# Patch embedding, attention and a ternary feed-forward layer on one core: the weighted values moved ahead of the column scores in each round

## The chip, the cores and the metric

The kernel runs on one core of one Trainium2 chip. The metric is the device time of one execution in microseconds (us); less is better. Engine names: PE is TensorE (matrix multiply), PEld its weight loads, DVE is VectorE, ACT is ScalarE, POOL is GpSimd, SP is the engine whose queue issues the DMAs.

## The reference

The input is 64 images of 3x224x224 and 64 texts of 32x256. Each image is cut into 196 patches of 16x16x3, each patch is multiplied with a 768x256 matrix, and a bias and a position are added. With the 32 text rows this makes sequences of 228 rows of 256. On them runs one transformer layer, cut here to its core:

```python
h = concatenate([patches(x) @ W_embed + b_embed + pos, txt], axis=1)   # 64 x 228 x 256
n = layernorm(h)
q, k, v = n @ Wq.T, n @ Wk.T, n @ Wv.T                                 # 16 heads of 16
probs = softmax(where(causal, -inf, q @ k.T / sqrt(16)))
h = h + (probs @ v) @ Wo.T + bo
h = h + ternary_linear(gelu(ternary_linear(layernorm(h), w_up)), w_down)   # 256 -> 1024 -> 256
```

A ternary linear layer divides its input by its root mean square and multiplies with the weights' signs, where a weight is over half of the mean absolute weight, and zero elsewhere.

## The kernel before, in words

The 64 images are worked on in 32 pairs. A software pipeline runs over steps t = 0 to 34; in step t pair t is embedded and gets its queries and keys, pair t-1 gets its values and row scores, pair t-2 finishes its attention, and pair t-3 is projected and goes through the feed-forward layer. Steps 3 to 31 have all four stages. A step has eight rounds, k = 0 to 7, and every engine walks through the same rounds with an order written out by hand. There is no planner; only the semaphores tie the engines together.

The attention of a pair is cut into eight groups of four heads. Each group is scored twice:

- **Row scores** (`scores_rows`): queries times keys with the mask added, 16 fp32 matmul instructions on tiles of 32 rows of the array (`score<-km,qm`) and 16 bf16 ones (`score<-cmask,idm`). DVE takes the row maxima from them (`maxima_unit`, L951 and L952).
- **Column scores** (`scores_columns`): the same products transposed, with the maxima folded into the queries, 16 instructions `score<-qm,km`, again on tiles of 32 rows. ACT takes the exponential (`exponential`, L674, tile `pr`), and POOL sets what lies above the diagonal to zero (`causal`, L1155).
- **Weighted values** (`weighted_values`): values times probabilities, 16 instructions `pvps<-pr,vp` with 114 contraction rows and 32 output rows each. Every second round ACT copies the result out (`unscaled`, L741, tile `raw`), DMAs repack it, and DVE divides by the sums (`collect`).

Row and column scores share one PSUM tile, `score`, of four banks. So the column scores of round k wait until DVE has read the row scores of round k, and the row scores of round k+1 wait until the exponential of round k has read the column scores:

```python
eng.wait_ge(*score_emptied(t, k, True))     # columns: v["max"] of this round's rows
eng.wait_ge(*score_emptied(t, k, False))    # rows: a["exp"] of the last columns
```

Everything else that PE does ("dense" work: `pixels`, `embed`, `hidden_rows`, `to_columns`, `queries_keys`, `values`, `projection`, `up`, `down`, `sum_squares`, `maxima_rows`) is laid by hand into the two stretches of a round. The first stretch lies between row scores and column scores, the second between column scores and the next row scores. In steps 3 to 31 they hold:

| round | first stretch | second stretch, behind the weighted values |
|---|---|---|
| 0 | projection | pixels 0 to 2 |
| 1 | values 0, pixels 3 to 5 | embed 0, first half |
| 2 | embed 0, second half, x2t | up 0 to 2 |
| 3 | up 3 to 7 | maxima_rows 0, embed 1 |
| 4 | hidden_rows, values 1 | down, 8 instructions |
| 5 | down, 16 | down, 16 |
| 6 | sum_squares, down, 16 | down, 8, and xt |
| 7 | queries_keys 0 | queries_keys 2 (ahead of the weighted values), maxima_rows 1 |

In round 7 the second half of `queries_keys` (2) needs a PSUM bank that ACT empties (`queries`, L699, tile `qm`). The weighted values of round k belong to the group whose column scores were made in round k-1. They wait for POOL's mask of that group (`p["mask"]`) and, in every second round, for the copy `raw` (`a["raw"]`). The probabilities have two buffers, and the exponential of a group waits for the weighted values of the group two before it. Nearly all matmuls are issued through one helper and appear under its line, L324.

Of the kernel before, what the change touches and what calls it, by code (L numbers as in the profile page):

```python
# [75 lines left out]
def build(nc, x, txt, w_embed, b_embed, pos, wqkvo, bo, w_upT, w_downT, out):  # L76
    with ExitStack() as ctx:
# [116 lines left out]
        def live(pair):  # L194
            return not isinstance(pair, int) or 0 <= pair < NPAIR

        def emptied(pair, name, k):

            m, back = DENSE.index((name, k)) - 3, 0
            while back < 3:  # L200
                if m < 0:
                    m, back = m + NDENSE, back + 1
                other, j = DENSE[m]
                if other != "spare":
                    before = pair + (lag(name, k) - back - lag(other, j))
                    if live(before):
                        if other == "qk":
                            return (a["km"], count(2, before, j // 2 + 1)) if j % 2 else (a["q"], count(4, before, j + 2))
                        return released[other], count(PER[other], before, j + 1)
                m -= 3  # L210
            return a["w"], 1
# [20 lines left out]
        def bank_of(name, k):  # L232
            return dense[:, DENSE.index((name, k)) % 3]
# [88 lines left out]
        def _(eng):  # L322
# [62 lines left out]
            def queries_keys(pair, k):  # L385

                ps = [bank_of("qk", k + j)[:, 0:T2] for j in range(2)]
                w_ = [[[z[:, j, c, (k // 2) * 128:(k // 2) * 128 + 128] for z in wa] for c in range(2)] for j in range(2)]
                if pair == 0 and k == 0:
                    eng.wait_ge(v["wa"], 1)  # L390
                for j in (1, 0):
                    eng.wait_ge(*emptied(pair, "qk", k + j))
                    for c in range(2):
                        if k == 0 and j == 1:
                            eng.wait_ge(a["xt"], count(2, pair, c + 1))
                        mm(ps[j], w_[j][c][0], aT[0][:, c], start=(c == 0), stop=False)
                        mm(ps[j], w_[j][c][1], aT[0][:, c], start=False, stop=False)
                for j in range(2):
                    for c in range(2):
                        if k == 0 and j == 0:  # L400
                            eng.wait_ge(v["xt"], count(2, pair, c + 1))
                        last = mm(ps[j], w_[j][c][0], aT[1][:, c], start=False, stop=(c == 1))
                    last.then_inc(pe["qk"], 1)
# [71 lines left out]
            def scores_columns(t, u, k):  # L475

                pair, q = columns_of(t, k)
                if not live(pair):
                    return
                b, r = divmod(q, 4)  # L480
                m, par = divmod(r, 2)
                buf = u if k < 5 else 1 - u
                if r == 0:
                    eng.wait_ge(v["mq"], count(2, pair, b + 1))

                eng.wait_ge(*score_emptied(t, k, True))
                for kb in range(2):
                    c0 = b * S + kb * R
                    for i in range(4):
                        last = mm(score[0:R, i, kb * S:S + kb * R], km[quad(i), buf, m, par, c0:c0 + R],  # L490
                                  qm[quad(i), par, buf, m, c0:b * S + S], start=True, stop=True,
                                  skip_group_check=True)
                last.then_inc(pe["st"], 1)
# [26 lines left out]
            def weighted_values(pair, par, gi):  # L520

                b, r = divmod(gi, 4)

                eng.wait_ge(p["mask"], count(16, pair, 2 * gi + 2))
                if pair == 0 and gi == 0:
                    eng.wait_ge(v["tbound"], 1)
                if gi == 0:

                    eng.wait_ge(a["v0"], count(2, pair, 2))

                if gi >= 2 and gi % 2 == 0:
                    eng.wait_ge(a["raw"], count(4, pair, gi // 2))
                elif gi == 0 and began(pair - 1):
                    eng.wait_ge(a["raw"], count(4, pair - 1, 4))
                P_ = pr[gi % 2]
                half = r % 2
                for kb in range(2):
                    for i in range(4):
                        last = mm(pvps[quad(i), half * S + kb * R:half * S + S],
                                  vp[:, par + 1 if b else 0, kb, 8 * (r // 2) + 2 * i + half],  # L540
                                  P_[:, i, kb * S:S + kb * R], start=(kb == 0), stop=(kb == 1),
                                  skip_group_check=True)
                last.then_inc(pe["pv"], 1)
# [11 lines left out]
            def step(t, hs):  # L555
                u = hs % 2
                A, Bm, Cc, Dd = live(t), live(t - 1), live(t - 2), live(t - 3)
                for k in range(8):
                    if Bm:
                        scores_rows(t, u, k)  # L560
                    if Dd and k == 0:
                        projection(t - 3)
                    if Bm and k == 1:
                        values(t - 1, 0)
                    if A and k == 1:
                        pixels(t, 3)
                        pixels(t, 4)
                        pixels(t, 5)
                    if A and k == 2:
                        embed(t, 0, 1)  # L570
                    if Dd and k == 2:
                        eng.wait_ge(a["xn2"], count(4, t - 3, 4))
                        to_columns(t - 3, "x2t", 0, xn)
                        to_columns(t - 3, "x2t", 1, xn)
                    if Dd and k == 3:
                        for m in range(3, 8):
                            up(t - 3, m)
                    if A and k == 4:
                        hidden_rows(t, 0)
                        hidden_rows(t, 1)  # L580
                    if Bm and k == 4:
                        values(t - 1, 1)
                    if Dd and k == 5:
                        down(t - 3, 0, 1)
                        down(t - 3, 0, 2)
                    if Dd and k == 6:
                        sum_squares(t - 3)
                        down(t - 3, 1, 1)
                        down(t - 3, 1, 2)
                    if A and k == 7:  # L590
                        queries_keys(t, 0)
                    scores_columns(t, u, k)
                    if A and k == 7:
                        queries_keys(t, 2)
                    pair, gi = (t - 2, k + 2) if k < 6 else (t - 1, k - 6)
                    if live(pair):
                        weighted_values(pair, u if k < 6 else 1 - u, gi)
                    if A and k == 0:
                        pixels(t, 0)
                        pixels(t, 1)  # L600
                        pixels(t, 2)
                    if A and k == 1:
                        embed(t, 0, 0)
                    if Dd and k == 2:
                        up(t - 3, 0)
                        up(t - 3, 1)
                        up(t - 3, 2)
                    if Bm and k in (3, 7):
                        maxima_rows(t - 1, k // 4)
                    if A and k == 3:  # L610
                        embed(t, 1, 0)
                        embed(t, 1, 1)
                    if t == 1 and k == 4:
                        eng.wait_ge(v["tsum"], 3)
                        mm(pvps[:, 0:3], onesf, tern[:, 0:3], start=True, stop=True).then_inc(pe["init"], 1)
                    if Dd and k == 4:
                        down(t - 3, 0, 0)
                    if Dd and k == 5:
                        down(t - 3, 0, 3)
                        down(t - 3, 1, 0)  # L620
                    if Dd and k == 6:
                        down(t - 3, 1, 3)
                    if A and k == 6:
                        eng.wait_ge(a["xn"], count(4, t, 4))
                        to_columns(t, "xt", 0, xn)
                        to_columns(t, "xt", 1, xn)

            steps(step, eng)


# [625 lines left out]
```

## Time and profile before

| | |
|---|---|
| median of 3 runs | 2014.7 us (2012.65 to 2017.67) |
| profiled execution, its own time | 2019.13 us |
| its span, first to last instruction | 2017.4 us |
| mean granted TensorE clock | 0.978 of full speed |
| PE busy | 1927.3 us, 96% of the span |
| PEld busy | 1574.9 us, 78% |
| DVE, ACT, POOL busy | 1465.9, 1312.9, 892.5 us |

All durations come from the profiled execution. A matmul's row in the timeline gives the start of the first instruction of the group, its length to the modelled end of the last, the names out<-in, the count, and, where the engine sat idle before it, how long and what ended the idle time. Modelled ends overlap the next start, so that the time a group takes from PE is read from start to start.

### The profile page before, as it was taken

The numbers are of one execution on the slowest core, as the hardware profiler recorded it, in microseconds if no ns is written. First come the engines' busy times: TensorE is split into PE (matmuls) and PEld (weight loads), VectorE is DVE, ScalarE is ACT, GpSimd is POOL, SyncE is SP. The second block draws the span as 40 slices with busy tenths as digits, with TensorE's granted clock in tenths as the row PEclk, the third lists the DMA queues.
The fourth block names the chain that finished last, engine by engine and source line by source line (L and its number), as shares of the span: only waits on it lengthen the run. The fifth ranks groups of instructions, "written<-read, shape, count | busy, mean of one in ns | idle before, by whom it ended". The sixth has DMA issues, their size and how long they took to land.

```text
span 2017.4 us, 59822 instructions
## 1 busy us (share of the span) xinstructions
PE 1927.3 (96%) x25090; PEld 1574.9 (78%) x25090; DVE 1465.9 (73%) x2717; ACT 1312.9 (65%) x1986; POOL 892.5 (44%) x1067
## 2 busy tenths in 40 slices
PE   4779999999999999999999999999999999999975
PEld 3668888888888888788888888888888888888754
DVE  3667778777777777777777777777777778777753
ACT  3347766666776676767667677666667766667652
POOL 1124444444444544444454444444454445444543
PEclk8789999999999999999999999999999999999987
DMA  5011111111111101111111111111111111010000
GB/s 149 15 46 41 50 55 50 35 45 44 53 50 55 50 27 53 41 55 50 53 47 31 47 49 51 54 50 35 45 45 52 50 55 50 30 51 17 30 29 24
DMA packets 66116, 93.72 MB, mean 46 GB/s; under 512 B 10082, under 2 KB 59718, under 8 KB 65592
## 3 DMA queue, kind: packets, MB, share of 16 engines
q1 hardware_dynamic: 65848, 89.90, 15.6%
q8 instruction: 199, 3.26, 0.7%
q14 instruction: 69, 0.57, 0.1%
HBM read 45.03 MB, written 14.94 MB: 30 GB/s over the span
## 4 chain that ended last, share of the span: by engine, by line
PE 90%; ACT 3%; DVE 3%; issue 2%; POOL 1%; DMA 1%; SPq 0%; DVEq 0%; POOLq 0%; ACTq 0%
PE dense L324 50%; PE score L324 21%; PE pvps L324 9%; PE dense L342 4%; PE dense L381 3%; ACT qm L699 2%; PE dense L552 2%; PE dense L370 1%; POOL acc L1174 1%; DMA borow<-bo 1%; DVE mx L952 1%; ACT pr L674 0%; DVE st L936 0%; DVE mx L951 0%; ACT xn L723 0%
## 5 line engine op out<-in xcount | busy, mean ns | idle before, releaser
L1155 POOL TENSOR_SCALAR_AFFINE_SELECT pr<-pr 114x456 f32<-114x456 f32 x512 | 310.8, 631 | 853.2 <-ACT pr L674 853.2
L674 ACT ACTIVATE pr<-score 114x1368 f32<-114x1368 f32 x256 | 335.6, 1311 | 301.3 <-PE score L324 301.0
L951 DVE TENSOR_REDUCE mx<-score 114x4 f32<-114x456 f32 x256 | 161.1, 629 | 260.3 <-PE score L324 259.7
L952 DVE TENSOR_REDUCE mx<-score 114x4 f32<-114x912 f32 x256 | 281.0, 1098 | 0.0
L324 PE MATMUL dense<-wdn,g 128*114 128x256 bf16 x1024 | 243.4, 283 | 2.0 <-ACT g L683 1.2
L324 PE MATMUL score<-qm,km 32*114 32x228 f32 (+1 forms) x4096 | 221.8, 331 | 18.7 <-DVE mx L952 15.4
L324 PE MATMUL dense<-wdn,gl 128*114 128x256 bf16 x1024 | 236.6, 276 | 0.0
L1174 POOL TENSOR_TENSOR acc<-acc,sq 128x456 f32<-128x456 f32 x192 | 222.4, 1158 | 19.0 <-POOL acc L1174 0.4
L324 PEld LDWEIGHTS score<-qm,km 32*114 32x114 f32 x4096 | 176.0, 175 | 69.4 <-issue 40.5
L324 PE MATMUL score<-km,qm 32*114 32x114 f32 (+1 forms) x4096 | 221.8, 331 | 7.5 <-ACT pr L674 6.7
L324 PE MATMUL pvps<-pr,vp 114*32 114x228 f32 (+1 forms) x4096 | 205.2, 318 | 1.0 <-ACT raw L741 0.6
L908 DVE RECIPROCAL rs<-rs 128x228 f32<-128x228 f32 x128 | 200.5, 1566 | 5.5 <-DMA cx<-raw 5.5
L324 PEld LDWEIGHTS score<-km,qm 32*114 32x114 f32 x4096 | 127.1, 175 | 60.1 <-issue 37.9
L324 PEld LDWEIGHTS pvps<-pr,vp 114*32 114x32 f32 x4096 | 108.5, 110 | 68.9 <-POOL pr L1155 10.9
L683 ACT ACTIVATE g<-dense 128x456 f32<-128x456 f32 x256 | 135.1, 553 | 29.9 <-PE dense L324 29.4
L324 PEld LDWEIGHTS dense<-wdn,g 128*114 128x114 bf16 x1024 | 137.3, 134 | 19.8 <-issue 16.3
L324 PE MATMUL dense<-pT_hi,we_hi 128*128 128x392 f32 x384 | 142.3, 371 | 3.8 <-DVE pT_lo L898 2.2
L691 ACT ACTIVATE sq<-g 128x456 f32<-128x456 f32 x256 | 142.2, 580 | 1.4 <-POOL acc L1174 1.4
L324 PE MATMUL dense<-xT_hi,wup 128*128 128x456 f16 x512 | 142.8, 361 | 0.1
L716 ACT ACTIVATE vp<-dense 114x512 f32<-114x512 f32 x64 | 41.1, 642 | 156.2 <-PE dense L324 156.2
L324 PE MATMUL dense<-xT_lo,wup 128*128 128x456 f16 x512 | 141.7, 359 | 0.0
L324 PEld LDWEIGHTS dense<-wdn,gl 128*114 128x114 f16 x1024 | 136.2, 133 | 0.0
(125 smaller groups left out, 4402.5 us busy)
## 6 DMA issues: line engine op xcount, KB each, us to landing
pix<-x SPq DMA_DIRECT2D x64, 588.0 KB
rs<-raw SPq DMA_DIRECT2D x256, 57.0 KB, 2.0
cx<-raw SPq DMA_DIRECT2D x256, 57.0 KB, 2.0
out<-h SPq DMA_DIRECT2D x64, 228.0 KB
h<-txt SPq DMA_DIRECT2D x32, 64.0 KB, 7.1
km<-wqkvo SPq DMA_DIRECT2D x1, 1024.0 KB, 13.7
h<-w_upT SPq DMA_DIRECT2D x1, 1024.0 KB, 14.1
km<-w_embed SPq DMA_DIRECT2D x1, 768.0 KB, 6.6
```

The source lines that it names most:

```text
L324: return nc.tensor.matmul(*args, **kw)
L342: last = nc.tensor.transpose(ps[:, i * PROWS:(i + 1) * PROWS], patches[:, ph, n], ident[0:PROWS, 0:PROWS])
L381: last = nc.tensor.transpose(ps[:, col(blk, b):col(blk, b) + R], src[:, c0:c0 + 128], ident[0:R, 0:R])
L674: act(pr[q % 2][:], score[0:R, :, 0:SW], ACT.Exp, scale=float(HD) ** -0.5).then_inc(a["exp"], 1)
L683: act(g[:, m], bank_of("up", m)[:, 0:T2], ACT.Gelu).then_inc(a["gelu"], 1)
L691: act(sq[:, m % 4], g[:, m], ACT.Square).then_inc(a["sq"], 1)
L716: act(dst, bank_of("v", k)[0:R, 0:2 * D].rearrange("p (e c) -> p e c", c=HD), ACT.Copy).then_inc(a["v0"], 1)
L908: nc.vector.reciprocal(rs[:, k % 2], rs[:, k % 2]).then_inc(v["rs"], 1)
L951: nc.vector.tensor_reduce(mx[:, m, 0, x:128:32], score[0:R, :, 0:R], AX.X, ALU.max)
L952: nc.vector.tensor_reduce(mx[:, m, 1, x:128:32], score[0:R, :, R:SW], AX.X, ALU.max).then_inc(v["max"], 1)
L1155: nc.gpsimd.affine_select(out=blocks, in_=blocks, compare_op=ALU.is_ge, fill=0.0, base=0, pattern=[[0, 4], [1, R]], channel_multiplier=-1) ...
L1174: tt(acc[:], sq[:, 0] if m == 1 else acc[:], sq[:, m % 4], ALU.add).then_inc(p["acc"], 1)
```

## The change

In each round PE now issues the weighted values ahead of the column scores instead of behind them. In round 7, where `queries_keys(t, 2)` stood between the two, both now stand ahead of it. The order on all other engines stays as it is, and so does every wait.

```diff
                     if A and k == 7:
                         queries_keys(t, 0)
+                    pair, gi = (t - 2, k + 2) if k < 6 else (t - 1, k - 6)
+                    if live(pair):
+                        weighted_values(pair, u if k < 6 else 1 - u, gi)
                     scores_columns(t, u, k)
                     if A and k == 7:
                         queries_keys(t, 2)
-                    pair, gi = (t - 2, k + 2) if k < 6 else (t - 1, k - 6)
-                    if live(pair):
-                        weighted_values(pair, u if k < 6 else 1 - u, gi)
                     if A and k == 0:
                         pixels(t, 0)
                         pixels(t, 1)
```

## Rows read from the trace of the kernel before

**Rows 1.** The page: span, and granted clock in 40 slices (tenths).
```profile
span 2017.4 us, 59822 instructions
...
PEclk8789999999999999999999999999999999999987
```

**Rows 2.** The chain that ended last, by engine.
```profile
PE 90%; ACT 3%; DVE 3%; issue 2%; POOL 1%; DMA 1%; SPq 0%; DVEq 0%; POOLq 0%; ACTq 0%
```

**Rows 3.** Waits of PE, 300 to 1800 us: us in total, times, longest.
```profile
PE dense L324 <- DVE pT_lo L898: 0.9, 2, 0.5
...
PE score L324 <- DVE mx L952: 0.2, 1, 0.2
```

**Rows 4.** Timeline of PE, round 4 of a full step to round 7.
```profile
1025.68 0.85 PE L324 MATMUL score<-qm,km 32*114 32x228 f32 x16
1026.46 0.79 PE L324 MATMUL pvps<-pr,vp 114*32 114x228 f32 x16
1027.18 0.32 PE L324 MATMUL dense<-wdn,g 128*114 128x256 bf16 x1
...
1028.20 0.86 PE L324 MATMUL score<-km,qm 32*114 32x114 f32 x16
...
1031.13 0.85 PE L324 MATMUL score<-qm,km 32*114 32x228 f32 x16
...
1037.87 0.85 PE L324 MATMUL score<-qm,km 32*114 32x228 f32 x16
...
1041.16 0.86 PE L324 MATMUL score<-km,qm 32*114 32x114 f32 x16
```

**Rows 5.** Timelines of ACT and of POOL in the same step, rounds 4 to 7.
```profile
1026.66 1.31 ACT L674 ACTIVATE pr<-score 114x1368 f32<-114x1368 f32 x1 [0.23 <-PE score L324]
...
1035.28 0.53 ACT L741 ACTIVATE raw<-pvps 128x456 f32<-128x456 f32 x1
...
1044.56 1.18 ACT L699 ACTIVATE qm<-dense,pmask 128x456 f32<-128x456 f32 x2 [1.04 <-PE dense L324]
...
1028.14 1.13 POOL L1155 TENSOR_SCALAR_AFFINE_SELECT pr<-pr 114x456 f32<-114x456 f32 x2 [2.31 <-ACT pr L674]
```

**Rows 6.** The chain in order of time, round 0: start, length, what.
```profile
1053.83 0.78 PE score L324 x16
1054.61 0.72 PE pvps L324 x16
1055.33 1.17 PE dense L342 x14
1056.49 1.02 PE score L324 x32
```

**Rows 7.** Timeline of PE in step 2, where the feed-forward work is missing.
```profile
118.32 0.85 PE L324 MATMUL score<-qm,km 32*114 32x228 f32 x16
...
120.75 0.86 PE L324 MATMUL score<-km,qm 32*114 32x114 f32 x16 [0.86 <-ACT pr L674]
...
123.60 0.85 PE L324 MATMUL score<-qm,km 32*114 32x228 f32 x16 [1.75 <-DVE mx L952]
...
126.10 0.53 PE L324 MATMUL dense<-pT_hi,we_lo 128*128 128x392 f32 x1
...
133.92 0.85 PE L324 MATMUL score<-qm,km 32*114 32x228 f32 x16
...
136.26 0.86 PE L324 MATMUL score<-km,qm 32*114 32x114 f32 x16 [0.77 <-ACT pr L674]
```

**Rows 8.** Timeline of PE's weight loads, round 7 of a full step.
```profile
1044.86 0.67 PEld L324 LDWEIGHTS score<-qm,km 32*114 32x114 f32 x16 [0.31 <-issue]
1045.78 0.19 PEld L324 LDWEIGHTS dense<-aT_hi,wa_hi 128*128 128x128 f32 x1 [0.26 <-ACT qm L699]
...
1048.46 0.55 PEld L324 LDWEIGHTS pvps<-pr,vp 114*32 114x32 f32 x16 [0.31 <-POOL pr L1155]
1049.18 0.40 PEld L552 LDWEIGHTS dense<-ident,mx 114*128 114x128 f32 x4 [0.17 <-issue]
```

## The prediction, made before the changed kernel had run

> **What bounds the kernel now.** I read the page first: the granted clock stands at nine tenths or more in nearly every slice [rows 1], so the durations below hold for the whole span. The chain that ended last is PE for 90% [rows 2]. The question is then whether PE ever waits in the middle. The list of waits over 300 to 1800 us says no: its largest entries for the matmuls are 0.9 us on DVE in all, and 0.2 us on the row maxima [rows 3]. It has no entry at all for the exponential. PE's own instruction stream sets the time, and every microsecond by which PE is made to wait goes into the result.
>
> So the question is not what the weighted values cost, since their 16 instructions are issued in either order, but what they cover. Each round has two hand-overs of the tile `score`. Between row scores and column scores DVE must take the maxima. Between column scores and the next row scores ACT must take the exponential. The weighted values lie in the second stretch now and will lie in the first.
>
> **What the hand-overs need.** Step 2 lacks the feed-forward work, and so it shows the needs bare. Column scores start at 133.92, the next row scores at 136.26 after a wait on ACT, 2.34 us apart; another pair gives 120.75 - 118.32 = 2.43 [rows 7]. A full step says the same from its parts: columns start at 1025.68, ACT begins at 1026.66 and takes 1.31 [rows 4, 5], which makes 0.98 + 1.31 = 2.29, and 0.05 to 0.14 of release. I take 2.34, upper end 2.43. The first hand-over needs 123.60 - 120.75 = 2.85 from row scores to column scores, ended by DVE [rows 7].
>
> **The first stretch has nothing to gain.** The shortest one of a full step I find in round 5, 1031.13 - 1028.20 = 2.93 [rows 4], and it is above 2.85; the 0.2 us of waits on the maxima [rows 3] are all that there is to win. The weighted values there cover nothing.
>
> **The second stretch loses 0.72 us of cover in each round.** The weighted values take 1027.18 - 1026.46 = 0.72 from start to start [rows 4], and 0.72 in the chain [rows 6]. What is left from the columns' start to the next row scores:
>
> - Round 4: 1028.20 - 1025.68 = 2.52 now [rows 4], 1.80 without them. ACT needs 2.34, so PE stalls 0.54 (0.63 by the upper end).
> - Round 0: 1056.49 - 1053.83 = 2.66 now [rows 6], 1.94 without. Stall 0.40 (0.49).
> - Round 6: 1041.16 - 1037.87 = 3.29 now [rows 4], 2.57 without: above 2.34 by 0.23, no stall. I read rounds 1, 2, 3, 5 and 7 in the same way; all have longer second stretches than round 6. In round 3 ACT is still at its gelus when the columns come, in either order.
>
> Together 0.94 us a full step, between 0.94 and 1.12.
>
> **Round 7 gives a little back.** There the columns start at 1044.86 and the next dense work's weights load at 1045.78, after 0.26 of idle loading that ended with ACT's copies `qm` [rows 8]; these ran from 1044.56 for 1.18, to 1045.74 [rows 5]. Columns take about 0.78 elsewhere (1026.46 - 1025.68 [rows 4]), so some 0.14 of the 0.92 are a wait. With the weighted values in front, the dense work could start no sooner than 1044.86 + 0.72 + 0.78 = 1046.36, when `qm` is long done, and the wait is gone. The move also saves one change of tile shape: weights for the weighted values wait 0.31 behind dense work [rows 8], and here they take over the place behind dense work that the columns have, with the same 0.31 [rows 8]. I put the two at 0.14 + 0.06 = 0.20; nothing at all is the lower end, and 0.26 + 0.31 = 0.57 the most that both idle times could hold.
>
> **The changes of tile shape in the other rounds.** The order dense, columns, values, dense becomes dense, values, columns, dense. The entry behind dense work costs the same 0.31 for both [rows 8]. The exit from values to dense has 0.17 of idle loading [rows 8]. Values straight ahead of columns, and columns straight ahead of dense work with nothing else in the way, do not occur in the rows. Bounds from the nearest: the exit of the columns lasts at most 1045.78 - 1044.86 = 0.92 with the wait in it [rows 8], against 0.78, so 0.14 dearer; and an exit that drops the 0.17 [rows 8] would be as much cheaper. I take zero, because each order has three changes and one is known to cost the same. If a twentieth of a microsecond were off in each of the 8 rounds of a step, that would be 0.4 us a step either way. The Trainium skill (TensorEngine Tiling (Array Packing), Key Properties) says that changing the tiling mode drains the engine; columns are tiles of 32 rows, weighted values tiles of 32 columns. The idle times of 0.17 and 0.31 fit it [rows 8]. By that rule both orders pay three drains in seven rounds, and round 7 pays four before and three after; it would leave the sum as it is.
>
> **What else is moved.** The exponential starts 0.72 later in every round against the row scores. Behind it on ACT stand `raw`, the normalizations and the squares. The nearest need of the moved weighted values is in round 6: `raw` ends at 1035.28 + 0.53 = 1035.81 [rows 5], 0.72 later now, and the values would start at 1037.87 instead of 0.78 behind it [rows 4]; 1.3 us are left. The masks: POOL ends round 4's at 1028.14 + 1.13 = 1029.27 [rows 5], later by 0.72 too, and round 5's values would start no sooner than 1031.13 [rows 4]; 1.1 us are left even without the stall. SP's repacking DMAs follow `raw`, by 0.6 us later at most in round 7, and DVE collects them rounds later. No DMA is moved past another. The tightest place is in round 3, where up 3 needs the bank that the first gelu empties; that gelu comes 0.72 later and just in time. I cost all this at nothing; the stalls of rounds 0 and 4 widen these margins.
>
> **The sum.** 0.94 - 0.20 = 0.74 us a full step, for 29 steps (3 to 31): 21.5 us. Step 2 and the steps from 32 on win on the first hand-over (1.75 us of wait on DVE before one column score [rows 7]) and lose on the second, 0.6 to 0.7 us each time; I put them together at +1, give or take 3. So +22 us: from the profiled execution's own 2019.1 to 2041, and from the median of 2014.7, which lies 0.2% below it, to 2037. The bounds: 29 x (0.94 - 0.57) = 11 and 29 x 1.12 = 32, and with 0.4 us a step for changes of shape on top, about 0 and 44.
>
> **Rivals.**
>
> - *Dearer changes of shape.* Values straight ahead of columns drain or reload worse than the other way round. For it: every change in the rows leaves loads idle, up to 0.31 [rows 8]. Against it: this is a change that both orders have. At 0.10 more a round, 8 x 29 x 0.10 = 23 on top: 2060. The Trainium skill (TensorE: Matmul & The Clock Gate, the part on packing small matmuls) has weight loads run ahead only into other row groups; the values' 114 rows touch all four groups, so the columns' loads would stand behind them, as the values' loads now stand behind the columns. That rule speaks for this rival no more than for the old order.
> - *No change: the stalls are absorbed.* It needs the row scores to be released earlier than 2.34, or PE to have hidden waits that shrink when it slips. For it: about nothing but PE's weight loads, which are idle a little ahead of each row score. Against it: a chain of PE without waits has nothing to give back [rows 2, 3]. 2010 to 2020.
> - *Faster.* The decisive place is the columns' way out: if dense work behind columns could load its weights without the 0.17 that it has behind values [rows 8], that is 8 x 29 x 0.17 = 39 won against 22 lost, 1998. It decides from 22 / 232 = 0.09 us a round on. Against it: the 0.92 of round 7 shows no short exit, though it holds a wait.
> - *The clock falls.* In step 2 it did: a 392-column matmul took 0.53 [rows 7]. It came after stalls of 0.86 and 1.75 us within 4 us; the scores right behind the stall of 0.86 still ran at their 0.86 [rows 7]. Stalls of 0.4 and 0.54, 28 us apart, are smaller. If it fell once a step for some 3 us of work at half clock, it would cost 1.5 x 29 = 44: 2080.
>
> **How the numbers follow.** Chances: forecast 0.73, dearer changes of shape 0.10, faster 0.06, absorbed 0.07, clock 0.04. For the forecast alone 2026 to 2048. The range for 8 in 10 reaches a little into the dearer case: 2024 to 2054. Within 0.3%, 6 us, is what a measurement of this kernel cannot tell from no change. Slower by more: 0.86 (forecast, dearer, clock, less a little that falls inside). Within: 0.08. Faster: 0.06.
>
> **What would show it.** In the changed profile, PE's waits over 300 to 1800 us should have a new entry, score on ACT `pr`, of some 24 us in about 50 times: 0.4 in round 0 and 0.5 in round 4 of each full step. Columns to row scores should read 2.34 to 2.43 there and about 2.57 in round 6. The wait of the loads on `qm` should be gone. PE's row scores to column scores should grow by 0.72 in each round. If columns to row scores in round 2 shortens by more or less than 0.72, the changes of shape have a price. I am wrong if PE waits on ACT without the time growing, or if the values wait for POOL's mask or for `raw`.

## The result, and the profile after

The changed kernel takes 2033.5 us (median of 4 runs, 2032.19 to 2036.18) against 2015.4 us before (4 runs): 1.0094 times as long, 95% interval 1.0073 to 1.0116. It is 18 us slower; the forecast was 22 us slower. The profiled execution took 2036.18 us, against 2019.13.

The page after, span, busy times and granted clock, and the chain by engine and by line:

```profile
span 2034.5 us, 59822 instructions
...
PE 1919.5 (94%) x25090; PEld 1573.6 (77%) x25090; DVE 1480.6 (73%) x2717; ACT 1310.8 (64%) x1986; POOL 887.5 (44%) x1067
...
PEclk8899999999999999999999999999999999999977
...
PE 88%; ACT 5%; DVE 2%; issue 2%; POOL 1%; DMA 1%; SPq 0%; ACTq 0%; DVEq 0%; POOLq 0%
PE dense L324 49%; PE score L324 23%; PE pvps L324 9%; ACT pr L674 4%; PE dense L381 3%; PE dense L342 2%; PE dense L370 1%; PE dense L552 1%; DMA borow<-bo 1%; POOL acc L1174 1%; ACT xn L723 1%; DVE mx L952 0%; DVE mx L951 0%; DVE st L936 0%; DVE h L973 0%
```

The clock did not fall: between 300 and 1800 us the granted clock is 1.00 in both profiles, and it dips only at the two ends [rows 1]. ACT went from 3% of the chain [rows 2] to 5%, and 4% is now the exponential, `pr` L674. PE's busy time did not grow (1919.5 us against 1927.3), so the new time is idle time.

Waits of PE over 300 to 1800 us, after, which answers to [rows 3]:

```profile
PE score L324 <- ACT pr L674: 22.2, 50, 0.5
```

That one line is the whole list. Between 300 and 1800 us lie 25 steps, so PE waits for the exponential twice a step, 0.44 us on the mean. (The list understates the loss: from start to start, in the table below, it is 1.03 us a step, and the list has 0.89.) The place is seen in the timelines. PE in rounds 4 to 6 of a full step, and ACT's exponential of round 4:

```profile
1027.10 0.79 PE L324 MATMUL pvps<-pr,vp 114*32 114x228 f32 x16
1027.82 0.85 PE L324 MATMUL score<-qm,km 32*114 32x228 f32 x16
1030.17 0.86 PE L324 MATMUL score<-km,qm 32*114 32x114 f32 x16 [0.47 <-ACT pr L674]
...
1040.53 0.85 PE L324 MATMUL score<-qm,km 32*114 32x228 f32 x16
1043.11 0.86 PE L324 MATMUL score<-km,qm 32*114 32x114 f32 x16
...
1028.80 1.31 ACT L674 ACTIVATE pr<-score 114x1368 f32<-114x1368 f32 x1 [0.92 <-PE score L324]
```

Columns start at 1027.82, ACT begins 0.98 later, takes 1.31, and the next row scores start 0.06 after its end: 2.35 us from start to start, where 2.52 were filled before [rows 4]. In round 6 the distance is 2.58, all of it filled. From row scores to column scores every round is longer by 0.69 to 0.73 (medians of 28 steps), as it must be when the weighted values move there. Round 0 in the chain, in order of time, which answers to [rows 6]:

```profile
1055.52 0.72 PE pvps L324 x16
1056.23 0.83 PE score L324 x16
...
1057.14 1.32 ACT pr L674
1058.46 0.14 issue
1058.60 1.09 PE score L324 x29
```

The chain leaves PE for ACT here; before it stayed on PE. Round 7 in PE's weight loads, which answers to [rows 8]:

```profile
1046.81 0.55 PEld L324 LDWEIGHTS pvps<-pr,vp 114*32 114x32 f32 x16 [0.31 <-issue]
1047.53 0.67 PEld L324 LDWEIGHTS score<-qm,km 32*114 32x114 f32 x16 [0.17 <-issue]
1048.31 0.19 PEld L324 LDWEIGHTS dense<-aT_hi,wa_hi 128*128 128x128 f32 x1
...
1050.71 0.54 PEld L552 LDWEIGHTS dense<-ident,mx 114*128 114x128 f32 x4
```

The wait on `qm` is gone, and so is one idle time of 0.31 ahead of the weighted values. The loads show what the new neighbours cost: 0.31 behind dense work, 0.17 from values to columns, and none listed from columns to dense work (by the rows 0.11 us: 1047.53 + 0.67 = 1048.20 to 1048.31). Before it was 0.31 and 0.17 [rows 8], and none is listed from columns to values in any full step. From start to start, over 300 to 1800 us, the columns take 0.78 to 0.79 us and the weighted values 0.72 in either order. The idle times have changed places, and their sum is the same.

The next table is worked out from the timelines of PE: the time from the start of one round's row scores to the next one's, in a full step near 400 us, for before, the changed kernel and the experiments below. The last column is the step, which I read from 28 successive steps; it is the same within 0.02 us in most of them.

| kernel | 0 | 1 | 2 | 3 | 4 | 5 | 6 | 7 | step |
|---|---|---|---|---|---|---|---|---|---|
| before | 6.71 | 7.16 | 7.53 | 10.24 | 5.99 | 6.33 | 6.64 | 8.55 | 59.15 |
| changed | 7.20 | 7.17 | 7.53 | 10.24 | 6.53 | 6.30 | 6.64 | 8.29 | 59.90 |
| e1: ahead in 0 and 4 | 7.19 | 7.17 | 7.53 | 10.24 | 6.53 | 6.33 | 6.64 | 8.57 | 60.20 |
| e2: ahead in the six others | 6.71 | 7.17 | 7.53 | 10.24 | 5.98 | 6.31 | 6.64 | 8.29 | 58.87 |
| e3: ahead in 7 | 6.72 | 7.16 | 7.53 | 10.24 | 5.98 | 6.33 | 6.64 | 8.27 | 58.87 |
| e4: behind in 7 | 6.72 | 7.16 | 7.53 | 10.24 | 5.98 | 6.33 | 6.64 | 8.28 | 58.88 |
| e5: changed, short exp | 6.82 | 7.37 | 7.53 | 10.23 | 6.15 | 6.30 | 6.64 | 8.29 | 59.33 |
| e6: before, short exp | 6.71 | 7.32 | 7.54 | 10.25 | 5.98 | 6.33 | 6.64 | 8.55 | 59.32 |
| e7: changed, down in 4 | 7.21 | 7.16 | 7.54 | 10.23 | 6.86 | 5.61 | 6.64 | 8.28 | 59.53 |

### The profile page after: what moved, and what is told of

Read it like the earlier page. It is cut to its first block, busy times and chain, and to the rows that moved or that the text cites. A ratio compares the mean times of both kernels' runs of the same rounds, so it can differ in the third digit from the quotient of the medians.

```text
span 2034.5 us, 59822 instructions
## 1 busy us (share of the span) xinstructions
PE 1919.5 (94%) x25090; PEld 1573.6 (77%) x25090; DVE 1480.6 (73%) x2717; ACT 1310.8 (64%) x1986; POOL 887.5 (44%) x1067
## 4 chain that ended last, share of the span: by engine, by line
PE 88%; ACT 5%; DVE 2%; issue 2%; POOL 1%; DMA 1%; SPq 0%; ACTq 0%; DVEq 0%; POOLq 0%
PE dense L324 49%; PE score L324 23%; PE pvps L324 9%; ACT pr L674 4%; PE dense L381 3%; PE dense L342 2%; PE dense L370 1%; PE dense L552 1%; DMA borow<-bo 1%; POOL acc L1174 1%; ACT xn L723 1%; DVE mx L952 0%; DVE mx L951 0%; DVE st L936 0%; DVE h L973 0%
## 5 line engine op out<-in xcount | busy, mean ns | idle before, releaser
L1155 POOL TENSOR_SCALAR_AFFINE_SELECT pr<-pr 114x456 f32<-114x456 f32 x512 | 303.4, 617 | 920.0 <-ACT pr L674 920.0
L674 ACT ACTIVATE pr<-score 114x1368 f32<-114x1368 f32 x256 | 336.0, 1313 | 393.5 <-PE score L324 390.9
```

Of the source, the lines that this page charges most:

```text
L674: act(pr[q % 2][:], score[0:R, :, 0:SW], ACT.Exp, scale=float(HD) ** -0.5).then_inc(a["exp"], 1)
L1155: nc.gpsimd.affine_select(out=blocks, in_=blocks, compare_op=ALU.is_ge, fill=0.0, base=0, pattern=[[0, 4], [1, R]], channel_multiplier=-1) ...
```

## The experiments

The two theories on record are A, lost cover (the row scores wait for the exponential where the second stretch is too short), and B, a price in each round for changing the shape of the tiles in the new order. Ratios are to the kernel before, run on the same chip.

**e1, ahead in rounds 0 and 4 only.**

Against the kernel before:

```diff
+                    pair, gi = (t - 2, k + 2) if k < 6 else (t - 1, k - 6)
+                    if live(pair) and k in (0, 4):
+                        weighted_values(pair, u if k < 6 else 1 - u, gi)
                     scores_columns(t, u, k)
                     if A and k == 7:
                         queries_keys(t, 2)
                     pair, gi = (t - 2, k + 2) if k < 6 else (t - 1, k - 6)
-                    if live(pair):
+                    if live(pair) and not (k in (0, 4)):
                         weighted_values(pair, u if k < 6 else 1 - u, gi)
```

> The weighted values stand ahead of the column scores in rounds 0 and 4 only; in all other rounds the order is that of before. Theory A (lost cover: the row scores of the next round wait for the exponential where the second stretch is too short): the same two stalls a full step as in the changed kernel, 22.2 us over 25 steps there, so 0.89 us a step and 29 x 0.89 = 26 us over before, near 2041 us, and above the changed kernel, because round 7's gain is missing. Rival B (each round with the new order pays for its changes of tile shape, 18 us spread over 8 rounds): 2 of 8 rounds, 4 to 5 us over before, near 2020 us.

Measured 2043.4 us against 2013.5, ratio 1.0156 (1.0131 to 1.0181): 30 us slower, and slower than the changed kernel. PE's waits, 300 to 1800 us:

```profile
PE score L324 <- ACT pr L677: 22.3, 50, 0.5
```

They are those of the changed kernel (the line is three further down). Two rounds of eight hold the whole loss, and more than the whole of it. B would have had 4 to 5 us.

**e2, ahead in the six other rounds.** The same edit with `k not in (0, 4)`.

> The weighted values stand ahead in rounds 1, 2, 3, 5, 6 and 7, and behind the column scores in rounds 0 and 4. Theory A: no stall on the exponential in a full step, and round 7's gain stays; the profile after has 4.32 us there between two points where before had some 0.25 more, so 29 x 0.25 = 7 us under before, near 2008 us. Rival B (price by round): 6 of 8 rounds, 13 to 14 us over before, near 2029 us.

Measured 2009.2 us against 2013.5, ratio 0.9979 (0.9963 to 0.9996). The wait on the exponential is absent from PE's list:

```profile
PE dense L324 <- DVE pT_lo L901: 0.9, 2, 0.5
```

The same exchange in six rounds is a little faster than before, so B is wrong as a price by round. A gave 2008. In the table only round 7 differs from before by more than 0.02 us.

**e3, ahead in round 7 only.** The same edit with `k == 7`.

> The weighted values stand ahead of the column scores in round 7 only, with queries_keys 2 behind both. Theory A: the five other moves of e2 are free, so this takes the same time as e2, some 7 us under before, near 2008 us. Rival B: round 7's part of a price, within 3 us of before or slower. If e2 and e3 differ by more than their uncertainty, moving the values in a round with long stretches has a price or a gain of its own.

Measured 2005.1 us against 2013.5, ratio 0.9963 (0.9947 to 0.9978). Its step is that of e2, 58.87 us. The medians of e2 and e3 lie 4 us apart, with intervals that overlap, and the profiled executions the other way round (spans 2002.6 and 2003.7 us). Most of the 4 us goes with the granted clock, which the runs have beside their times (see the sum, below): at the same clock e2, e3 and e4 lie 8.2, 8.8 and 9.5 us under the kernel before, where 29 steps at 0.28 make 8.1. So the five moves in rounds 1, 2, 3, 5 and 6 are free within what this measurement tells.

**e4, behind in round 7, but ahead of `queries_keys` 2.**

```diff
                     scores_columns(t, u, k)
+                    pair, gi = (t - 2, k + 2) if k < 6 else (t - 1, k - 6)
+                    if live(pair) and k == 7:
+                        weighted_values(pair, u if k < 6 else 1 - u, gi)
                     if A and k == 7:
                         queries_keys(t, 2)
                     pair, gi = (t - 2, k + 2) if k < 6 else (t - 1, k - 6)
-                    if live(pair):
+                    if live(pair) and k != 7:
                         weighted_values(pair, u if k < 6 else 1 - u, gi)
```

> The order of before in all rounds, but in round 7 the weighted values follow the column scores directly and queries_keys 2 comes last (columns, values, queries_keys 2). Theory A (round 7 gains because the values fill the wait for ACT's copies qm, and one change of tile shape is saved): it does not matter which of the two comes first, so the same as e3, near 2008 us. Rival C (the gain comes from having the values ahead of the columns, for instance a cheaper way from columns into dense work): no gain here, near 2015 us.

Measured 2005.5 us against 2013.5, ratio 0.9964 (0.9951 to 0.9978), the same as e3. Round 7's weight loads, e4:

```profile
386.72 0.67 PEld L324 LDWEIGHTS score<-qm,km 32*114 32x114 f32 x16 [0.31 <-issue]
387.50 0.55 PEld L324 LDWEIGHTS pvps<-pr,vp 114*32 114x32 f32 x16
388.22 0.19 PEld L324 LDWEIGHTS dense<-aT_hi,wa_hi 128*128 128x128 f32 x1 [0.17 <-issue]
...
390.61 0.55 PEld L552 LDWEIGHTS dense<-ident,mx 114*128 114x128 f32 x4
```

The gain of round 7 does not come from the exchanged order, and rival C falls. It comes from putting the values next to the columns and ahead of `queries_keys` 2, by which the wait on `qm` and one entry of 0.31 vanish. No run has the one without the other, but the rows divide the gain: from columns to dense work it is 0.78 where 0.93 stood before, so the wait had 0.14 to 0.15, and the remaining 0.12 to 0.14 go with the entry that is saved.

**e5 and e6, a shorter exponential, in the changed kernel and in the one before.**

```diff
-                act(pr[q % 2][:], score[0:R, :, 0:SW], ACT.Exp,
+                act(pr[q % 2][:, :, R:SW], score[0:R, :, R:SW], ACT.Exp,
...
+            for z in pr:
+                eng.memset(z[:], 1.0)
```

> The changed kernel, whose exponential leaves out the first 114 of each 342 columns (912 instead of 1368 elements a partition; those probabilities keep the 1.0 that is set once at the start, so the output is not the reference's). From 0.54 us for 456 elements and 1.31 for 1368 the short one should take 0.92, 0.39 less. Theory A: the row scores are released 0.39 earlier, the stalls of 0.89 us a full step fall to about 0.1, and with a few us at the ends the time falls by 23 to 27 us, to near 2009 us, under the kernel before. Rival B (price of the changes of tile shape): nothing changes in PE's order, so at most the few us at the ends, near 2029 us.

> The same short exponential in the kernel before, as a control. Theory A: PE never waits for the exponential in a full step there, so only the ends gain: 3 to 6 us, near 2009 us, about the same as the changed kernel with the short exponential or some us above it for round 7's sake. Rival B: the same here, and 18 us less than the changed kernel with the short exponential.

Measured: e5 2013.7 us and e6 2012.8, both against 2013.9; ratios 1.0010 (0.9994 to 1.0025) and 0.9999 (0.9984 to 1.0015). The exponential takes 0.93 us instead of 1.31. The changed kernel gives back nearly all of its 18 us, the one before gains at most 1, and the two stand level: the loss hung on how long ACT takes. B had 18 us between them. But both were to come out some us below the kernel before, near 2009, and did not. Its timeline of PE, round 4 and then round 0, shows one part of why:

```profile
1017.14 0.85 PE L324 MATMUL score<-qm,km 32*114 32x228 f32 x16
1019.10 0.86 PE L324 MATMUL score<-km,qm 32*114 32x114 f32 x16
...
1045.10 0.85 PE L324 MATMUL score<-qm,km 32*114 32x228 f32 x16
1047.15 0.86 PE L324 MATMUL score<-km,qm 32*114 32x114 f32 x16
```

Round 4 has 1.96 from columns to row scores where 1.80 are filled, and round 0 has 2.05 where 1.94 are: 0.27 us a step is left, not 0.1. The forecast had started from the 0.89 of the list of waits, not from the 1.03 that the stalls cost from start to start, and the list does not show stalls this short. The other part stands in round 1, which is 0.20 us longer in e5 than before, and 0.16 in e6, too. Step by step, DVE in round 0 and the weight loads ahead of `values` 0 in round 1 of e6:

```profile
459.57 0.44 DVE L1059 TENSOR_SCALAR ve<-mv 114x4 f32<-114x4 f32 x1
459.92 0.16 DVE L1060 COPY ve<-mv 114x4 f32<-114x4 f32 x1
459.99 1.50 DVE L900 TENSOR_TENSOR pT_lo<-dense,pT_hi 128x420 fp32r<-128x420 f32 x3
...
460.62 0.17 PEld L324 LDWEIGHTS dense<-wa_hi,aT_hi 128*114 128x114 f32 x1 [0.18 <-DVE pT_lo L900]
```

and the same DVE instructions in the kernel before:

```profile
463.13 0.27 DVE L1057 TENSOR_SCALAR ve<-mv 114x4 f32<-114x4 f32 x1
463.31 0.15 DVE L1058 COPY ve<-mv 114x4 f32<-114x4 f32 x1
463.38 1.50 DVE L898 TENSOR_TENSOR pT_lo<-dense,pT_hi 128x420 fp32r<-128x420 f32 x3
```

A DVE instruction on 4 elements takes 0.44 instead of 0.27 us, what stands behind it comes later by that, and `values` 0 waits for the bank that `pT_lo` frees. POOL's mask, two `AFFINE_SELECT`s of about 0.6 us whose starts lie 0.54 apart, runs beside it in both, and the short exponential lets it start earlier against DVE. In 22 of 25 steps of the kernel before, the stretched instruction ends 0.61 or 0.62 us after POOL's first select starts, as that select ends; in e6 it ends at 1.15 or 1.16, as the second does, in 22 steps; in e5 it is the copy behind it that is stretched, to 0.56 from 0.16, and ends 0.63 or 0.64 after the first starts. In the changed kernel, where POOL starts after it, it takes 0.17. So a small DVE instruction that starts beside a select ends with it; that the select holds it is argued from these times, and no run takes POOL away. In e6 the 0.17 to 0.18 us a step make some 5 us, about what a shorter exponential was forecast to win at the ends.

**e7, more work in round 4's second stretch, in the changed kernel.**

```diff
                     if Dd and k == 5:
-                        down(t - 3, 0, 1)
                         down(t - 3, 0, 2)
...
                     if Dd and k == 4:
                         down(t - 3, 0, 0)
+                        down(t - 3, 0, 1)
```

> The changed kernel with one quarter of the down projection of block 0 (8 instructions, 0.95 us) moved from the first stretch of round 5 to the end of the second stretch of round 4. Theory A: round 4's stretch is then 1.80 + 0.95 = 2.75 us, above the 2.34 that the exponential needs, and its stall of 0.47 is gone. Round 5's first stretch becomes 2.91 + 0.72 - 0.95 = 2.7 from row scores to column scores, under the 2.85 that the maxima need, so 0.15 to 0.2 comes back as a wait on DVE. Together 0.3 us a step, 8 to 10 us under the changed kernel, near 2024 us. Rival B: PE's changes of shape are as many as in the changed kernel, no change, near 2033 us.

Measured 2025.3 us against 2013.9, ratio 1.0049 (1.0030 to 1.0068): about half of the loss is gone, and the step is 0.38 us over that of before instead of 0.75. PE's waits over 300 to 1800 us, and its timeline from round 4's columns to round 5's:

```profile
PE score L324 <- ACT pr L674: 10.3, 25, 0.4
...
1022.97 0.85 PE L324 MATMUL score<-qm,km 32*114 32x228 f32 x16
1025.64 0.86 PE L324 MATMUL score<-km,qm 32*114 32x114 f32 x16
...
1027.68 0.79 PE L324 MATMUL pvps<-pr,vp 114*32 114x228 f32 x16
1028.58 0.85 PE L324 MATMUL score<-qm,km 32*114 32x228 f32 x16
```

The wait on the exponential is left once a step, in round 0; round 4's is gone, since its 2.67 us are filled with work. The price is in round 5: values to columns take 0.90 instead of 0.72, 0.18 of wait, and row scores to columns 2.94. Theory A had 2.85 there and 0.15 to 0.2. The hand-over to DVE thus needs 2.94 in round 5, as much as the kernel before had filled, so that first stretch had no margin. Work moved from one hand-over of the tile uncovers the other.

## Why the prediction was right

- **PE's stream sets the time, and nothing waits.** Right for the full steps: each loss that the table shows went into the result. At the two ends PE waits in both kernels.
- **The hand-over needs 2.34 to 2.43 us.** Right: 2.35 in round 4, and 1058.60 - 1056.16 = 2.44 in round 0. The lower value holds for one, the upper for the other. Both come from step 2 [rows 7], where the release after ACT's end was 0.14 one time (119.30 + 1.31 to 120.75) and 0.05 the other (134.90 + 1.31 to 136.26). What decides between the two is not shown. ACT in the kernel before:

```profile
119.30 1.31 ACT L674 ACTIVATE pr<-score 114x1368 f32<-114x1368 f32 x1 [0.39 <-PE score L324]
...
134.90 1.31 ACT L674 ACTIVATE pr<-score 114x1368 f32<-114x1368 f32 x1 [0.23 <-PE score L324]
```

- **0.72 of cover lost in each round, felt only in rounds 0 and 4.** Right: the table has +0.49 and +0.54, forecast 0.40 and 0.54. e1 has these two alone and loses 1.05 us a step; e2 has the six others and loses nothing. The upper end of the need, 2.43, would have given round 0's 0.49.
- **Nothing to gain in the first stretch.** Right but for 0.03 in round 5. The need there is 2.94 by e7, not the 2.85 of step 2; that the stretch was just long enough was closer than the forecast knew.
- **Round 7 gives 0.20 back.** 0.26, with the mechanism of the forecast; e3 and e4 have it alone, 0.28. The wait on `qm` was 0.14 as forecast, and the saved change of shape about 0.12 where 0.06 were put.
- **Changes of tile shape cost zero.** Right. The two places that the rows did not show have 0.17 and no idle loading. The drain of the Trainium skill (TensorEngine Tiling (Array Packing), Key Properties) fits what the loads show at some changes, 0.17 to 0.38 of idle time; at others, out of the columns above all, none is listed, so the rows neither show it there nor exclude it. e2 shows that five more rounds in the exchanged order cost nothing.
- **The sum.** 0.49 + 0.54 - 0.26 - 0.03 + 0.01 = 0.75 a full step, forecast 0.74; 29 steps make 21.8 us. The medians differ by 18.1, the profiled executions by 17.1. Three things stand between.
  - *Hiccups.* The kernel before has six rounds, in five of its 28 steps, that are 0.13 to 0.71 us longer than usual, 2.75 us together, with single waits of up to 0.5 us on DVE or "issue" [rows 3]; the changed kernel has one of 0.16. From the first full step to the last its 28 steps take 1677.3 us against 1659.0, which is 18.3 more where 28 x 0.75 = 21.0. A stall in round 0 hides them: four of the six are in round 1, and so are the 1.07 us of them in e2, which has round 1's new order without the stall, while e1, which has the stall with round 1's old order, keeps 0.15. This term was put at nothing.
  - *The ends*, put at +1, give about -2 in the profiled executions (17.1 less 18.3 and less 0.76 of the last full step), and that is the sum of two larger ones. The first full step starts 7.8 us earlier (152.8 us against 160.5); that is the first hand-over, as forecast, and also the clock, granted at 0.91 of full speed over the first 150 us against 0.85: e4 and e6, with the order of before in the ramp, start it near 156 at 0.90 and 0.89. The tail takes 5.8 us more. There the weighted values, now first, make the columns wait with them for POOL's mask and for `raw`:

```profile
1952.11 1.37 PE L324 MATMUL pvps<-pr,vp 114*32 114x228 f32 x16 [2.79 <-POOL pr L1155]
...
1975.99 1.37 PE L324 MATMUL pvps<-pr,vp 114*32 114x228 f32 x16 [4.24 <-ACT raw L741]
```

  The kernel before has 1.0 us of such waits in its tail, the changed one 7.2. That the two ends cancel is luck.
  - *The clock of the single runs.* The 29 runs of before beside e1 to e4 go from 2006.4 us at a mean granted clock of 0.986 to 2019.6 at 0.979, and a line through them leaves 1.1 us. Against that line the four runs of the changed kernel, taken apart from them, lie 19 to 24 us higher, 22 on the mean, and e1 30. So of the 4 us by which 18.1 falls short of the forecast 22, most goes with the clock of the runs compared.
- **Rivals.** Dearer shapes, a cheaper way out of the columns, absorption and the clock: e1 to e4 rule out the first two, e5 to e7 tie the loss to the exponential, and the clock stays at 1.00 in the middle. A small part of "absorbed" did happen, with the hiccups, about 3 us.
- **Waits for the mask or for `raw`.** None in the middle of the run, as said. But the prediction named such waits as a sign of being wrong, and at the end of the run they are there, 7.2 us (above), and in the ramp 2.3: "I cost all this at nothing" holds for the full steps only. In round 3 ACT is done with its gelus before it can start on the columns, 0.46 us early; the forecast had it still busy there, without harm (below).

## What to carry to other kernels

When two engines hand one buffer back and forth, ask of each piece of work which hand-over it covers, and compare from start to start what the stretch holds with what the hand-over needs; a ramp or a tail, where cover is missing, shows that need bare. Work moved from a stretch with 2.5 us and a need of 2.35 to one that is long enough costs its full length less the small margin, though no engine does more. Where the margin is there, as in six rounds of this kernel, the order is free, and the one place worth moving is where an existing wait can be filled: e3 and e4 beat both kernels at 0.996 (0.995 to 0.998). Where cover is missing anyway, in the tail, the group that is issued first decides what the next one waits for.

## What the runs showed of the hardware

ACT's table load waits with the instruction that it serves. In round 3 of the changed kernel, the same in 31 steps, ACT's last gelu ends at 1019.61, and the load for the exponential starts when the column scores are ready:

```profile
1019.04 0.57 ACT L683 ACTIVATE g<-dense 128x456 f32<-128x456 f32 x1
1020.07 1.28 ACT L674 ACT_TABLE_LOAD   x1 [0.46 <-PE score L324]
1021.36 1.31 ACT L674 ACTIVATE pr<-score 114x1368 f32<-114x1368 f32 x1
```

So the wait for the column scores also holds back 1.28 us of loading; no run here loads the table ahead of it. In the kernel before, the scores are ready first, and the load follows the gelu at once (1018.18 to 1018.20). Round 3's second stretch is long enough: the exponential ends at 1022.67 and the next row scores start at 1023.64. With a second stretch shorter than about 3.6 us (0.97 + 1.28 + 1.31 and the release, an estimate from these rows; it has 4.54), that round would have had a stall of its own.

The idle time of weight loads at a change of tile shape depends on the pair and not on the order as a whole. Over 25 steps of either kernel, into columns and into weighted values alike, it is 0.38 behind `up`, 0.31 behind `queries_keys`, 0.18 behind `down`, and none is listed behind the other dense work; it is 0.17 out of the weighted values into whatever follows, and none is listed out of the columns (0.11 by the rows).
